# Cross-attention over 64 keys: the mask added on 64 rows at a time, ahead of keys and queries

## The reference, cut to what matters

```
Q = heads(query @ w_q.T + b_q); K = heads(key @ w_k.T + b_k); V = heads(value @ w_v.T + b_v)
scores = Q K^T / sqrt(16)
scores = where(mask[:, None] == 0, -1e9, scores)
ctx = softmax(scores) V
out = ctx @ w_o.T + b_o + query
out = layernorm(out) * ln_gamma + ln_beta
```

## Time and profile before

| | us |
|---|---|
| median of 3 runs | 155.9 |
| lowest and highest | 155.34, 156.6 |
| profiled execution, its own time | 155.9 |
| profiled execution, its span | 154.0 |

### The profile page before, as it was taken

How to read it: one execution, slowest core, us unless ns; L and a number is a source line. 1 busy time by engine, 2 the same in 40 slices (tenths; PEclk the granted TensorE clock), 3 DMA queues, 4 the chain that set the end, 5 groups by cost and what they waited for, 6 DMA issues and landing times.

```text
span 154.0 us, 2935 instructions
## 1 busy us (share of the span) xinstructions
PE 136.3 (89%) x1008; PEld 85.4 (55%) x1008; DVE 125.3 (81%) x232; ACT 94.1 (61%) x166; POOL 112.3 (73%) x107
## 2 busy tenths in 40 slices
PE   0799897978999999999999999999999999999600
PEld 0677755554566646665656565655565455468400
DVE  0296958578879699978997799969998999999991
ACT  3349988867683757297729854783669555380420
POOL 6003748368996069899989999899909989879680
PEclk9999999999999999999999999999999999999965
DMA  5999735999999846208500760018300360200307
GB/s 138 352 302 271 183 88 175 283 304 284 333 237 304 189 135 222 69 0 200 213 2 0 152 261 0 0 34 237 144 0 2 50 227 0 107 33 0 136 2 272
DMA packets 10079, 22.88 MB, mean 149 GB/s; under 512 B 1616, under 2 KB 1872, under 8 KB 10064
## 3 DMA queue, kind: packets, MB, share of 16 engines
q1 hardware_dynamic: 9344, 21.50, 48.9%
q10 hardware_dynamic: 720, 1.19, 2.1%
HBM read 14.82 MB, written 4.19 MB: 123 GB/s over the span
## 4 chain that ended last, share of the span: by engine, by line
PE 67%; DVE 16%; issue 4%; ACT 4%; POOL 4%; DMA 3%; DVEq 1%; POOLq 0%
PE ps_w L402 12%; PE ps_w L357 12%; PE ps_s L436 10%; PE ps_s L465 9%; PE ps_w L491 8%; DVE nmax L750 7%; PE ps_s L442 4%; DVE stat L803 4%; PE ps_s L449 3%; DMA ctx_t<-ctxT 3%; PE ps_w L308 2%; PE ps_w L414 2%; POOL y L994 2%; POOL y L991 2%; PE ps_s L330 1%
## 5 line engine op out<-in xcount | busy, mean ns | idle before, releaser
L750 DVE TENSOR_REDUCE nmax<-ps_w 128x8 f32<-128x512 f32 x56 | 37.7, 683 | 14.1 <-PE ps_w L402 13.5
L649 ACT ACTIVATE probs<-ps_s 128x512 f32<-128x512 f32 x64 | 32.9, 599 | 13.5 <-PE ps_s L449 13.5
L926 POOL TENSOR_TENSOR xt_l<-xt_sb,xt_h 128x1024 fp32r<-128x1024 f32 x7 | 16.6, 2372 | 22.9 <-ACT xt_h L610 17.9
L402 PEld LDWEIGHTS ps_w<-k_half,q_mask 128*128 128x128 f32 x112 | 16.9, 188 | 25.1 <-DVE nmax L750 19.3
L402 PE MATMUL ps_w<-k_half,q_mask 128*128 128x256 f32 x112 | 27.3, 331 | 3.0 <-DVE nmax L750 2.5
L491 PE MATMUL ps_w<-wo_sb,cn 128*128 128x256 f32 x112 | 29.0, 387 | 0.3 <-issue 0.3
L491 PEld LDWEIGHTS ps_w<-wo_sb,cn 128*128 128x128 f32 x112 | 19.4, 189 | 5.8 <-issue 2.5
L617 ACT ACTIVATE q_sb<-ps_w,con 128x512 f32<-128x512 f32 x13 | 8.9, 686 | 21.7 <-PE ps_w L357 21.7
L962 POOL TENSOR_TENSOR x_sb<-x_sb,brow 128x1024 f32<-128x1024 f32 x8 | 19.0, 2375 | 2.3 <-DMA x_sb<-x 2.1
L770 DVE STREAM_TRANSPOSE turned<-ps_s 128x1024 f32<-128x1024 f32 x16 | 19.8, 1240 | 0.2 <-PE ps_s L465 0.2
L991 POOL TENSOR_TENSOR y<-y,brow 128x512 f32<-128x512 f32 x13 | 16.6, 1279 | 4.1 <-ACT y L662 3.8
(11 more groups left out here) (78 smaller groups left out, 197.3 us busy)
## 6 DMA issues: line engine op xcount, KB each, us to landing
m_sb<-maskT SPq DMA_DIRECT2D x32, 128.0 KB, 6.8
x_sb<-x SPq DMA_DIRECT2D x8, 512.0 KB, 5.1
xt_sb<-xT SPq DMA_DIRECT2D x7, 512.0 KB, 7.0
q_mask<-mask SPq DMA_DIRECT2D x24, 128.0 KB, 4.0
out<-y SPq DMA_DIRECT2D x6, 512.0 KB, 3.6
xt_sb<-xT SPq DMA_DIRECT2D x2, 256.0 KB, 5.1
q_mask<-mask SPq DMA_DIRECT2D x8, 64.0 KB, 2.1
out<-y ACTq DMA_DIRECT2D x2, 256.0 KB, 2.2
```

The source lines that it names most:

```text
L402: mm = pe.matmul(max_bank(c, i)[:, half * 256:half * 256 + 256], q_mask[:, c % 2, half, j, t * P:(t + 1) * P], k_half[:, b % 2, half, j].r ...
L649: act.activation(probs[:, g % 2, quad], ps_s[:, quad], ACT.Exp).then_inc(e_done, 1)
L750: dve.tensor_reduce(nmax[:, c % 2, t].rearrange("p (q r) -> p q r", r=32)[:, :, 2 * j:2 * j + 2], max_bank(c, i).rearrange("p (q h k) -> p ...
```

## The change

The mask is kept with all 64 keys on 64 rows, on partitions 0 to 63 and again on 64 to 127: `m_sb` and `mask` lose the axis of two halves, and have 512 elements a partition where they had 1024. `load_mask` issues 2 DMAs where it issued 4, of 128 KB each. `m_first` goes; chunk 0's `q_mask` is made from `m_sb`, and `load_mask(0)` stands where the load of `m_first` stood. `copy_mask` and `copy_first_mask` issue 2 DMAs of 64 rows where they issued 4 of 32 rows, with the same bytes. `key_rows` is 128 elements a partition and not 256. On PE, `scores_and_mask` begins with the mask: 4 products of 64 rows (quads 0 and 2 from rows 0 to 63, quads 1 and 3 from rows 64 to 127), then the 4 products of keys and queries. The wait for `mask_done` stands ahead of both.

```diff
--- before.py
+++ after.py
@@ -37,7 +37,7 @@
 IDENT, PAIR_BLOCK, HALF_BLOCK = 0, P, P + 2
 SELECT = HALF_BLOCK + 4
 KEY_ROWS = SELECT + 4
-BIAS = KEY_ROWS + 2 * KEYS
+BIAS = KEY_ROWS + KEYS
 CONSTS = BIAS + 4
 
 
@@ -62,7 +62,7 @@
         wq_h = sb("wq_h", [P, PC, D], F32R)
         wq_l = sb("wq_l", [P, PC, D], F32R)
 
-        key_rows = sb("key_rows", [P, 2, 2, KEYS], F32R)
+        key_rows = sb("key_rows", [P, 2, KEYS], F32R)
         select = sb("select", [P, 2, 2, KEYS], F32R)
         kt = sb("kt", [P, 2, BATCHES, KEYS])
 
@@ -76,10 +76,8 @@
         xt_h = sb("xt_h", [P, 2, PC, CHUNK], F32R)
         xt_l = sb("xt_l", [P, 2, PC, CHUNK], F32R)
 
-        m_sb = sb("m_sb", [P, NI, 2, CHUNK], I32)
-        mask = sb("mask", [P, NM, 2, CHUNK], F32R)
-
-        m_first = sb("m_first", [P, CHUNK], I32)
+        m_sb = sb("m_sb", [P, NI, CHUNK], I32)
+        mask = sb("mask", [P, NM, CHUNK], F32R)
         q_sb = sb("q_sb", [P, NQ, 2, CHUNK])
 
         q_mask = sb("q_mask", [P, 2, 2, 2, CHUNK], F32R)
@@ -109,7 +107,7 @@
         in_con, in_ctx, in_wk, in_wq, in_wv, in_wo, in_rows = (sem(n) for n in (
             "in_con", "in_ctx", "in_wk", "in_wq", "in_wv", "in_wo", "in_rows"))
         in_first = [sem(f"in_first{d}") for d in range(PC)]
-        in_bv, in_mfirst, mfirst_done = sem("in_bv"), sem("in_mfirst"), sem("mfirst_done")
+        in_bv, mfirst_done = sem("in_bv"), sem("mfirst_done")
         in_xt = [sem(f"in_xt{i}") for i in range(2)]
         in_mask = [sem(f"in_mask{i}") for i in range(NI)]
         in_x = [sem(f"in_x{i}") for i in range(3)]
@@ -224,9 +222,8 @@
             def load_mask(c):
                 if c >= NI:
                     sp.wait_ge(mask_done, masks_done(c - NI))
-                for quad in range(QUADS):
-                    sp.dma_start(m_sb[quad_rows(quad), c % NI], maskT[c].rearrange("(a k) n -> k a n", a=2)
-                                 ).then_inc(in_mask[c % NI], 16)
+                for half in range(2):
+                    sp.dma_start(m_sb[rows(half), c % NI], maskT[c]).then_inc(in_mask[c % NI], 16)
 
             def load_x(c):
                 if c >= 3:
@@ -237,18 +234,17 @@
                 sp.wait_ge(mask_done, masks_done(c))
                 if c >= 2:
                     sp.wait_ge(max_done, HALVES * (c - 1))
-                for quad in range(QUADS):
-                    r = quad_rows(quad)
-                    sp.dma_start(q_mask[r, c % 2, 1 - quad // 2].bitcast(F32),
-                                 mask[r, c % NM, quad % 2].bitcast(F32).unsqueeze(1).to_broadcast([32, 2, CHUNK])
+                for half in range(2):
+                    r = rows(1 - half)
+                    sp.dma_start(q_mask[r, c % 2, half].bitcast(F32),
+                                 mask[r, c % NM].bitcast(F32).unsqueeze(1).to_broadcast([64, 2, CHUNK])
                                  ).then_inc(mk_in[c % 2], 16)
 
             def copy_first_mask(j, landed):
                 sp.wait_ge(mask_done, masks_done(1))
-                for quad in range(QUADS):
-                    r = quad_rows(quad)
-                    sp.dma_start(q_mask[r, 1, 1 - quad // 2, j].bitcast(F32), mask[r, 1, quad % 2].bitcast(F32)
-                                 ).then_inc(landed, 16)
+                for half in range(2):
+                    r = rows(1 - half)
+                    sp.dma_start(q_mask[r, 1, half, j].bitcast(F32), mask[r, 1].bitcast(F32)).then_inc(landed, 16)
 
             def store(c):
                 sp.wait_ge(bet_done, 2 * (c + 1))
@@ -262,11 +258,9 @@
             sp.dma_start(wk_sb[:], wk).then_inc(in_wk, 16)
             load_first_xt(0)
             load_first_xt(1)
-            for half in range(2):
-                sp.dma_start(m_first[rows(half)], maskT[0]).then_inc(in_mfirst, 16)
+            load_mask(0)
             load_xt(1)
             sp.dma_start(wv_sb[:], wv).then_inc(in_wv, 16)
-            load_mask(0)
             load_mask(1)
             load_xt(2)
             sp.dma_start(brow[:, 0:1], bias_rows[:, 0:1].to_broadcast([P, 1, D])).then_inc(in_bv, 16)
@@ -367,16 +361,16 @@
                     if c == 0:
                         pe.wait_ge(mfirst_done, 2)
                     elif c == 1:
-                        pe.wait_ge(mk_first, 16 * QUADS)
+                        pe.wait_ge(mk_first, 32)
                     else:
-                        pe.wait_ge(mk_in[c % 2], 16 * QUADS * (c // 2 + c % 2))
+                        pe.wait_ge(mk_in[c % 2], 32 * (c // 2 + c % 2))
 
                     pe.wait_ge(khalf_done, 2 if c == 0 else 4 * (b + 1))
                     pe.wait_ge(kid_done, 2 if b == 0 else 4)
                 if (c, i) == (0, TILES):
                     pe.wait_ge(khalf_done, 4)
                 elif (c, i) == (1, TILES):
-                    pe.wait_ge(mk_in[1], 16 * QUADS)
+                    pe.wait_ge(mk_in[1], 32)
                 if t == 0:
                     pe.wait_ge(qdir_done, 2 * (2 * c + j + 1))
 
@@ -430,17 +424,17 @@
                     if g == 1:
                         pe.wait_ge(kpair_done, 2)
                     pe.wait_ge(qe_done, g + 1)
+                if g:
                     pe.wait_ge(e_done, QUADS * g)
+                pe.wait_ge(mask_done, masks_done(c))
+                for quad in range(QUADS):
+                    r = rows(quad % 2)
+                    pe.matmul(ps_s[:, quad], key_rows[r].rearrange("p h k -> p (h k)"), mask[r, c % NM],
+                              start=True, stop=False)
                 for quad in range(QUADS):
                     r = quad_rows(quad)
                     pe.matmul(ps_s[:, quad], k_pair[r, b, j].rearrange("p h k -> p (h k)"), q_sb[r, c % NQ, j],
-                              start=True, stop=False)
-                pe.wait_ge(mask_done, masks_done(c))
-                for a in range(2):
-                    for quad in range(QUADS):
-                        r = quad_rows(quad)
-                        pe.matmul(ps_s[:, quad], key_rows[r, a].rearrange("p h k -> p (h k)"), mask[r, c % NM, a],
-                                  start=False, stop=False)
+                              start=False, stop=False)
 
             def scores_less_max(c, j):
                 pe.wait_ge(neg_done, c + 1)
@@ -675,8 +669,8 @@
             first_queries_out(1)
             queries_out(0, 0)
             queries_out(0, 1)
-            act.activation(key_rows[:], con[:, KEY_ROWS:KEY_ROWS + 2 * KEYS].rearrange("p (a k) -> p a k", a=2)
-                           .unsqueeze(2).to_broadcast([P, 2, 2, KEYS]), ACT.Copy).then_inc(const_done, 1)
+            act.activation(key_rows[:], con[:, KEY_ROWS:KEY_ROWS + KEYS].unsqueeze(1).to_broadcast([P, 2, KEYS]),
+                           ACT.Copy).then_inc(const_done, 1)
             act.activation(select[:].rearrange("p j h k -> p (j h) k"),
                            con[:, SELECT:SELECT + 4].unsqueeze(2).to_broadcast([P, 4, KEYS]),
                            ACT.Copy).then_inc(const_done, 1)
@@ -837,14 +831,14 @@
                                   ALU.add).then_inc(dve_bet_done, 1)
 
             def first_mask_values():
-                dve.wait_ge(in_mfirst, 32)
+                dve.wait_ge(in_mask[0], 32)
                 for half in range(2):
                     r = rows(1 - half)
-                    dve.tensor_scalar(q_mask[r, 0, half], m_first[r].unsqueeze(1).to_broadcast([64, 2, CHUNK]), 0.0, -BIG,
+                    dve.tensor_scalar(q_mask[r, 0, half], m_sb[r, 0].unsqueeze(1).to_broadcast([64, 2, CHUNK]), 0.0, -BIG,
                                       ALU.is_equal, ALU.mult).then_inc(mfirst_done, 1)
 
             def mask_values(c):
-                dve.wait_ge(in_mask[c % NI], 16 * QUADS * (c // NI + 1))
+                dve.wait_ge(in_mask[c % NI], 32 * (c // NI + 1))
                 dve.tensor_scalar(mask[:, c % NM], m_sb[:, c % NI], 0.0, -BIG,
                                   ALU.is_equal, ALU.mult).then_inc(mask_done, 1)
 
@@ -927,7 +921,7 @@
                                    ALU.subtract).then_inc(xl_done, 1)
 
             def mask_values(c):
-                pool.wait_ge(in_mask[c % NI], 16 * QUADS * (c // NI + 1))
+                pool.wait_ge(in_mask[c % NI], 32 * (c // NI + 1))
                 pool.wait_ge(mask_done, c)
                 if c >= NM:
                     pool.wait_ge(s_done, PAIRS * (c - NM + 1))
@@ -1064,8 +1058,7 @@
     for h in range(2):
         consts[row, PAIR_BLOCK + h] = row % 32 // DK == h
     consts[row, HALF_BLOCK + row % 64 // DK] = 1
-    for a in range(2):
-        consts[row, KEY_ROWS + KEYS * a + 32 * a + row % 32] = 1
+    consts[row, KEY_ROWS + row % KEYS] = 1
     for j in range(2):
         for h in range(2):
             for quad in range(QUADS):
```

## The result

The changed kernel took 159.46 us (median of 4 runs, 157.74 to 159.69) against 156.03 us, a ratio of 1.0212 with a 95% interval of 1.0167 to 1.0256. Timed again in more rounds it took 158.03 us (6 runs, 157.76 to 158.47) against 155.54, a ratio of 1.0145 (1.0107 to 1.0183). It is slower, by 2.5 to 3.4 us.

The account below looks back on a forecast made before the run. PE was taken to set the pace from the second group to the last chunks. 13 exposed groups at +0.20 us give +2.6, all else 0, so 155.9 + 2.6 = 158.5 us, range 156.3 to 159.8.

Parts of the forecast that it names:

- What one group costs: PE, each group's scores: one more change of row count (64 to 32) with a bare load, +0.20 us, bounds -0.03 and +0.23.
- The pull-ahead of loads to other row groups: PE: loads for quads 0 and 1 could pass the mask product on rows 64 to 127; group then costs about +0.10 us.
- the values' 3.4 us for one product after another: PE: values' 16 instructions take 1.09 us, not 3.4, taken as sign that 64-row products on two halves run side by side.
- In how many groups: Of 16 groups, 0, 13 and 15 have cover; the other 13 pay on the chain: 13 x 0.20 = +2.6 us.
- 0.29 us of cover: Group 15: values end at 134.92, DVE turns them at 135.21, so its extra 0.20 us would not show.
- Group 0 and group 13: Covered groups: group 0's selection waits for `neg` (0.32 us), group 13's maxima wait for DVE (0.86 us).
- POOL, DVE, DMAs: 0: Work saved off PE's chain (POOL's masks about 9 us, shorter DVE masks, fewer DMA issues) changes the time by 0.
- PE's waits of 2.5 us for the maxima: PE's longest sum of idle waits, for DVE's maxima, with none for POOL in view: sign that PE sets the pace.
- Rival 1: No slower: PE changes from 64 to 32 rows without waiting, `k_pair` loads beside the last mask round; 155.5 us, chance 0.09.
- rival 2: Half a change: PE waits but the load is covered, or the reverse; +0.10 us a group, 157.2 us, chance 0.12.
- rival 3: The halves run one after another: four mask rounds, not two, some 0.66 us a group; about 165 us, chance 0.05.
- rival 4: The start or POOL was the bound: saved DMA, DVE and POOL work outweighs PE's loss; 154.0 us, chance 0.06.

Follow-up runs that it names:

- The order alone: Kernel before with its eight 32-row mask products and their wait moved ahead of keys and queries: 155.73 us against 155.54, ratio 1.0017.
- two changes: Changed kernel with its four 64-row mask products put back between keys and queries and the selection: 160.81 us, ratio 1.0325.
- one half for all: Changed kernel with all four mask products taken from rows 0 to 63: 164.18 us, ratio 1.0552.
- the two POOL runs: Changed kernel with POOL making each mask twice, 158.19 us against 158.03; kernel before with POOL making half of four chunks' masks, 155.60 against 155.67.
- POOL twice: Changed kernel in which POOL makes each of its five masks twice, first into a spare buffer: 158.19 us against the changed kernel's 158.03.
- the two with masks beside values: Changed kernel with mask products moved up behind the values: for ten groups (2, 4 to 12) 160.14 us, for the six even ones alone 159.15 us.
- POOL half: Kernel before with POOL making only the first half of the keys' masks for chunks 4 to 7: 155.60 us against 155.67, ratio 0.9994.

## Why the prediction was right

The forecast was 158.5 us; the two measurements are 159.46 and 158.03, both within 156.3 to 159.8. The first one's excess over the forecast, 0.96 us, is no error of the sum for the steps: its median lies between two runs (159.39 and 159.53) in which 1.1 to 1.6 us more than otherwise lay outside the span. The sum had nothing for that part, and that 159.46 still fell under 159.8 is luck. Without such runs the difference is 158.03 - 155.54 = 2.5 us, where 2.6 was forecast.

*What one group costs.* 0.20 us was forecast, 1.97 - 1.77 = 0.20 came. Its parts came too: `k_pair`'s first load starts 0.66 us behind the masks' first and is bare. The order alone (0), two changes (0.40) and one half for all (0.66) leave the change of shape as the only cause for the 0.2. The price can be followed in the start times: two mask rounds and the way to `k_pair` take 0.66 us, which is 2 x 0.23, the bare load of 0.10 ahead of the masks and 0.10 behind them in which nothing starts; `k_pair`'s own bare load then adds the second 0.10 to what one group pays. The Trainium skill's page "TensorEngine Tiling (Array Packing)", section Key Properties, has the engine drained when the mode changes. All these runs agree with it: behind a round that takes 0.23 us, the first load and product of the new shape start only 0.32 to 0.36 us after that round's start. The pull-ahead of loads to other row groups, which spoke for half the price, did not show across a change: the load port is idle for 0.37 us there. My case for it was weak besides, since quad 2's mask product runs on rows 0 to 63 while quad 3's runs on rows 64 to 127, so that no rows are free. And the values' 3.4 us for one product after another said nothing about the two halves: they are 8 tiles at once in two rounds (from 133.83 on and from 134.28 on), and one half after the other would be four rounds. The conclusion held, as one half for all showed.

*In how many groups.* 13 was forecast and 13 it was, but one of them is another. I had given group 15 0.29 us of cover, since DVE's `turned` at 135.21 starts that long after the end of PE's values. (In PE's order the values that stand behind group 15's selection are group 14's, which group 15's scores push back; group 15's own come at 137.64.) That is no slack. In the timelines of the changed kernel, PE and then DVE, it stands again:

```profile
136.06 1.09 PE L459 MATMUL ps_s<-probs,v_bd 64*32 64x512 f32 x16
```

```profile
137.44 1.25 DVE L764 STREAM_TRANSPOSE turned<-ps_s 128x1024 f32<-128x1024 f32 x1
```

The values end at 137.15 and `turned` starts at 137.44, the same 0.29 although all came 2.2 us later, and three groups earlier it is 117.67 + 1.09 to 119.04, 0.28, with DVE idle for 0.22 us before it. It is the time from PE's end to DVE's start. Group 15's cost passed on in full (DVE's `turned` went from +2.04 to +2.23). In return group 3, which I had counted, was covered. Ahead of the first output, PE waited in the trace before for `cn`; this is the stretch in that trace, PE first and then DVE:

```profile
42.36 0.50 PE L402 MATMUL ps_w<-k_half,q_mask 128*128 128x256 f32 x2
43.13 1.10 PE L491 MATMUL ps_w<-wo_sb,cn 128*128 128x256 f32 x4 [0.27 <-issue]
```

```profile
42.31 0.71 DVE L783 STREAM_TRANSPOSE cn<-div_t 128x512 f32<-128x512 f32 x1
```

`cn` ends at 43.02. The two maxima products at 42.36 hold PE for 0.34 us where the next product is ready (46.71 to 47.05 in the same trace), so PE had nothing to do from about 42.70 to 43.13. "issue" named no releaser there, and I had passed over it. In the changed kernel the maxima behind group 3 come 0.32 us later than before, and the output behind them only 0.13 (43.26), as `cn` does (43.15): group 3's cost went into that wait. Two errors of one group each, of opposite sign, left the sum right. That the count came out is luck.

*Group 0 and group 13* were covered as forecast: group 0's selection still waited for `neg`, and group 13's 0.20 us vanished in DVE's run of maxima.

*POOL, DVE, DMAs: 0.* POOL's 8.5 us less (18.2 to 9.7 for the masks) bought nothing, in either direction. PE's waits of 2.5 us for the maxima, from which I argued, are its longest behind its first product; the longest of all, 4.7 us, is the one for the first load ahead of it. ACT's `key_rows` went from 0.42 to 0.31 us and DVE's masks from 0.69 to 0.42, not to half. The loads' share of the sum wasn't tried alone: the DMAs and the start were told apart from the rest only by PE's times, which at group 0 differ as much between two profiles of one kernel as between kernels.

*The rivals.* Rival 1 and rival 2 fall with the loads; rival 3 was made real by one half for all, at 164.18 us where I had worked out about 165; rival 4 falls with the two POOL runs.

## What to carry to other kernels

Count, along PE's order, how often the shape of the tile changes, in rows or in columns: each change to a shape of 128 columns cost 0.09 to 0.13 us in which nothing starts and a bare load of 0.10 in this kernel, whatever the products themselves cost, so half the products in another shape can be dearer than twice as many in the shape of their neighbours. Where an engine is nearly full, ask who waits for it before counting its relief as a gain. Before products are moved to where their shape fits, ask what they wait for there (0.46 us for the score banks) and whom they push back (0.69 us for `cn`). And a constant gap between a producer's end and a consumer's start, found at other places of the same pair, is latency and no cover.

## What was not expected

The prediction counted changes of rows alone. The column count of a tile matters as its row count does: from 64 x 32 to 64 x 128 took the same 1.02 us from start to start as from 64 x 32 to 128 x 128.

The time outside the span was 1.5 to 2.0 us in almost all runs, but 2.99 to 3.43 us in 5 of the 36 runs of the six kernels that keep the mask on 64 rows (the changed one, masks between, one half, POOL twice and the two with masks beside values). It was never over 2.0 us in the 69 runs of the three with masks on 32 rows (before, order alone, POOL half). What makes it is open, and it wasn't tried.
